# A decoder layer on one core: attention and feed-forward in one block, the first pair's front among the last turns of attention

## The chip, the core and the metric

The kernel runs on one core of a Trainium2 chip. Time is microseconds (us) of one execution on the device; the number compared is the median of the runs. A core has five engines with queues of their own: TensorE (PE in the rows; PEld is its loading of weights), VectorE (DVE), ScalarE (ACT), GpSimd (POOL) and SyncE (SP), which issues the transfers here. They meet only at semaphores: `need(engine, semaphore, count)` lets an engine wait there until the semaphore has that count.

## The reference, cut

16 sequences ("blocks") of 128 tokens and 256 channels go through three residual steps: causal attention with a second, geometric attention mixed in per head; a WKV recurrence whose keys are the normalised rows and whose values are the context `ctx_2048`; and a feed-forward part with a Hadamard rotation, 8-bit activations and ternary weights.

```python
x = x + attn_ref(layernorm(x), Wq, Wk, Wv, Wo, head_scales)       # 8 heads, 2 key heads, width 32
x = x + xattn_ref(16, 128, 256, time_decay, time_first, layernorm(x), ctx_2048)
x = x + ffn_ref(layernorm(x), w_gate, w_up, w_down)               # 256 -> 1024 -> 256

def h_bitlinear(x, w):
    xq = act_quant(fwht(x))         # Hadamard, then 127 / max|x| per token, rounded
    return einsum('bsh,oh->bso', xq, weight_quant(w))
# ffn: h_bitlinear(silu(gate) * up, w_down), gate and up by h_bitlinear of the same rows
```

## The kernel before, in words

Everything lies in SBUF: `x_res` holds all 16 blocks and is updated in place. The program is two blocks of code, one behind the other; at the change every engine waits for all the others.

The first block is attention and the WKV step (WKV is called context here). It runs in **turns**: in turn r, block r is in its first stage (f: transposes, L476, and q/k/v, L514), block r-1 in the second (m: scores L459 and L467, transposed scores L483 and L490, row maxima L639, transposed row data L496 to L499, geometric bounds L663 to L696, geometric scores L563), block r-2 in the third (b: value products L552, output product L586, residual L776, and then the statistics of the next normalisation), block r-3 in the fourth (c: normalisation L645, transposes L523, exponentials L383 and L386, products with values on GpSimd), and block r-4 in the last (d: two scans L652 and L656, additions L702 and L707, ScalarE's logarithm and exponential L415 and L418, product L771, transposes L597, residual L795). VectorE has a stage e ahead of these, one block further. The functions `body` of each engine spell out the order; `pipeline` calls them for 20 turns (VectorE 21), fully unrolled. Turns 16 to 19 have ever fewer stages: 17 has b, c and d, 18 c and d, 19 d alone.

ScalarE also turns the feed-forward weights ternary, a piece a turn (`ternary`, L341 and L344), and GpSimd takes roots by a power of -1/2 (L283, L327, L893). VectorE casts the large Hadamard matrix (L759) in turn 16.

The second block is the feed-forward part, in **passes** over 8 pairs of blocks. In pass r, pair r is in its front f, pair r-1 in m, r-2 in h, r-3 in b. The front is a chain over all engines: statistics on VectorE (L1170 to L1180), root and shift on GpSimd (L893, L895), normalised rows on ScalarE (L949), four transposes on TensorE (L1058), a copy on ScalarE (L959), the Hadamard transform (L1069, into `hx`), the largest value and its factors on VectorE (L1198 to L1213), rounding on ScalarE (L973, L977) and the diagonal of scales on GpSimd (L905), the way back on TensorE (L1089, L1092), and two copies on ScalarE (L988, L990). m is four column blocks j: gate and up products (L1008), the scaled gate on VectorE (L1111), the silu on ScalarE (L921, which has another activation table than the first block's exponentials), the product (L1120) and a sum and difference (L1125, L1126), split into a high part on ScalarE (L927) and a low one on GpSimd (L884). h is the 1024-wide Hadamard (L1022) and its maximum (L1133); b is the rounding (L932, L1031, L938), the down product (L1037) and the last residual (L1160). Pass 0 has the front of pair 0 only.

Of the kernel before, what the change touches and what calls it, by code (L numbers as in the profile page):

```python
# [14 lines left out]
P = 128  # L15
# [16 lines left out]
PEEL = 6  # L32
# [6 lines left out]
def need(eng, sem, count):  # L39

    if isinstance(count, int) and count <= 0:
        return
    eng.wait_ge(sem, count)
# [10 lines left out]
def upto(count, n):  # L54

    return min(count, n) if isinstance(count, int) else count


def pipeline(eng, n, stages, peeled, body):

    at = lambda u: (u, u % 2) if 0 <= u < n else None
    for r in range(peeled):
        body(*(at(r - s) for s in range(stages)))
    if peeled < n:
        with eng.Fori(peeled // 2, n // 2) as j:
            for half in range(2):
                body(*((2 * j + half - s, (half - s) % 2) for s in range(stages)))
    for r in range(n, n + stages - 1):
        body(*(at(r - s) for s in range(stages)))


def decoder_layer(nc, t, out):
    with ExitStack() as ctx:
# [31 lines left out]
        unround_c = sb("unround_c", [P, 1])  # L105

# [41 lines left out]
        with ExitStack() as ph:  # L148
# [4 lines left out]

            had_f = ph.enter_context(nc.sbuf_tensor("had_f", [P, FQ * 512], F32))
            w_junk = had_f[:, :]
            pick_f = ph.enter_context(nc.sbuf_tensor("pick_f", [40, H * P], F32))
            hs_in = ph.enter_context(nc.sbuf_tensor("hs_in", [P, REP], F32))
            head_mix = ph.enter_context(nc.sbuf_tensor("head_mix", [P, REP], F32))
            w_o_raw = ph.enter_context(nc.sbuf_tensor("w_o_raw", [P, REP, C], F32))
            st6 = ph.enter_context(nc.sbuf_tensor("a_st6", [P, NB, 6], F32))  # L160
            mv = ph.enter_context(nc.sbuf_tensor("a_mv", [P, NB, 2], F32))
            ve = ph.enter_context(nc.sbuf_tensor("a_ve", [P, NB], F32))
            rstd = ph.enter_context(nc.sbuf_tensor("a_rstd", [P, NB], F32))
# [6 lines left out]
            split_k = sa("a_split_k", [P, 2 * KVH * 4 * DH], F32R)  # L170
            dq = sa("a_dq", [P, 2 * H * 3])
            proj_d = sa("a_proj_d", [P, 2 * H])
            qkT = sa("a_qkT", [P, 1024], F32R)
# [10 lines left out]
            g_diag = sa("a_g_diag", [40, H * P])  # L184
            e_s = sa("a_e_s", [P, H * P])
            e_g = sa("a_e_g", [P, H * P])
# [41 lines left out]

            block = ph.enter_context(nc.Block())

# [587 lines left out]
        with ExitStack() as ph:  # L818
# [50 lines left out]
            def _(sp):  # L869
# [4 lines left out]
                for i in range(2):  # L874
                    sp.wait_ge(s_y[i], 16 * NP)

# [413 lines left out]
```

## Time and profile before

| what | value |
|---|---|
| three runs | 465.57, 466.85, 467.7 us; median 466.85 |
| the profiled execution | 464.53 us |
| its span, first to last instruction | 462.6 us |
| mean granted TensorE clock | 0.919 of 2.4 GHz |
| busy: TensorE, VectorE, ScalarE, GpSimd | 383.4, 331.9, 258.3, 152.0 us |

A row of a timeline has the start in us, the duration, engine, line of the program, operation and shapes, and in brackets how long the engine idled ahead of it and who ended that. Rows of several instructions (x4) give the first start and the time to the last end. A row of a table of stretches has from and to, the length, and the busy time (with instructions) of TensorE, its weight loads, VectorE, ScalarE and GpSimd; then the granted clock, the share of the transfer engines and GB/s. A clock of 0.50 is the lower of two levels, 1.2 GHz, and 1.00 is 2.4 GHz.

### The profile page before, as it was taken

The page shows a single profiled execution, that of the slowest core. Times are in us where ns is not written, and L with a number is a line of the kernel's source. Part 1 is how long each engine was busy: PE and PEld are TensorE (multiplying, and loading weights), DVE is VectorE, ACT ScalarE, POOL GpSimd, SP SyncE. Part 2 cuts the span into 40 slices and gives each one's busy share as a digit, 9 for nine tenths or more (in the row PEclk, how much of TensorE's full clock was granted, in tenths as well). Part 3 has the DMA queues.
Part 4 walks back from the last instruction along what each step waited for, and adds up shares of the span by engine and source line. Part 5 has one row for each costly group of instructions (what it writes and reads, how often), then busy time and mean ns, then how long its engine had stood idle before and what let it go on. Part 6 is the DMA issues. An engine that isn't in the chain of part 4 may idle for free. (4 is left out here: it accounts for less than half of the span.)

```text
span 462.6 us, 7493 instructions
## 1 busy us (share of the span) xinstructions
PE 383.4 (83%) x2290; PEld 252.8 (55%) x2306; DVE 331.9 (72%) x865; ACT 258.3 (56%) x482; POOL 152.0 (33%) x161
## 2 busy tenths in 40 slices
PE   2578899999999999999997714778999999989795
PEld 1345455565554665555643302456777777768573
DVE  4374769877779787797877362568889898897742
ACT  1133676456775667756575222555675585755642
POOL 1221345334553335443341111133433333332310
PEclk9776999999999999999998566569999999999998
DMA  8930003000000000000000000000000000000001
GB/s 233 314 118 1 0 2 104 11 13 11 14 0 13 12 13 13 12 2 11 13 13 11 0 1 2 0 0 0 3 13 11 24 11 14 13 12 24 11 25 34
DMA packets 13642, 13.14 MB, mean 28 GB/s; under 512 B 2004, under 2 KB 12884, under 8 KB 13476
## 3 DMA queue, kind: packets, MB, share of 16 engines
q1 hardware_dynamic: 13604, 12.67, 9.1%
q8 instruction: 19, 0.31, 0.3%
q14 instruction: 19, 0.16, 0.1%
HBM read 10.57 MB, written 2.10 MB: 27 GB/s over the span
## 5 line engine op out<-in xcount | busy, mean ns | idle before, releaser
L884 POOL TENSOR_TENSOR c_h_lo<-c_hb,c_h_hi 128x512 fp32r<-128x512 f32 x32 | 40.8, 1274 | 72.0 <-ACT c_h_hi L927 66.7
L1022 PE MATMUL wide<-had,c_h_hi 128*128 128x512 f32 x128 | 54.0, 422 | 7.5 <-ACT c_q2T L938 7.5
L1022 PE MATMUL wide<-had,c_h_lo 128*128 128x512 f32 x128 | 51.2, 400 | 0.0
L1008 PE MATMUL wide<-c_q_T,w_tern_all 128*128 128x256 bf16 x256 | 38.3, 292 | 8.3 <-DVE c_hh L1120 6.9
L296 POOL TENSOR_TENSOR a_qk<-a_rot_c,a_rot_s 128x320 f32<-128x320 f32 x16 | 15.4, 962 | 72.6 <-DVE a_rot_s L677 72.6
L302 POOL TENSOR_TENSOR a_split_q<-a_qk,a_split_q 128x256 fp32r<-128x256 f32 x16 | 33.8, 2111 | 15.3 <-ACT a_split_k L394 15.3
L921 ACT ACTIVATE c_sl<-c_z 128x512 f32<-128x512 f32 x32 | 20.1, 628 | 29.4 <-DVE c_z L1111 29.3
L776 DVE TENSOR_TENSOR x_res<-x_res,bank 128x256 f32<-128x256 f32 x16 | 6.8, 422 | 40.9 <-PE bank L597 36.2
L1008 PEld LDWEIGHTS wide<-c_q_T,w_tern_all 128*128 128x128 bf16 x256 | 24.2, 103 | 20.7 <-DVE c_hh L1120 9.3
L586 PE MATMUL bank<-w_o,a_att 128*128 128x256 f32 x128 | 33.3, 405 | 1.9 <-issue 1.1
L563 PE MATMUL wide<-a_g_diag,a_row_sb 40*128 40x512 f32 x64 | 31.7, 615 | 2.6 <-DVE a_g_diag L696 2.6
L1022 PEld LDWEIGHTS wide<-had,c_h_hi 128*128 128x128 f32 x128 | 24.6, 192 | 14.0 <-issue 9.3
L327 POOL TENSOR_TENSOR b_rstd<-b_ve,neg_half 128x1 f32<-128x1 f32 x16 | 8.8, 552 | 66.1 <-DVE b_ve L812 66.1
L1111 DVE SCALAR_TENSOR_TENSOR c_z<-wide,w_scale,c_s_row 128x512 f32<-128x512 f32 x32 | 23.8, 743 | 7.7 <-PE wide L1008 7.0
L1120 DVE TENSOR_TENSOR c_hh<-wide,c_sl 128x512 f32<-128x512 f32 x32 | 22.1, 691 | 9.2 <-ACT c_sl L921 9.2
L1133 DVE TENSOR_REDUCE c_am<-wide 128x1 f32<-128x1024 f32 x16 | 19.5, 1218 | 12.6 <-PE wide L1022 12.6
L586 PEld LDWEIGHTS bank<-w_o,a_att 128*128 128x128 f32 x128 | 24.1, 198 | 7.4 <-DVE a_att L765 2.5
L1022 PEld LDWEIGHTS wide<-had,c_h_lo 128*128 128x128 f32 x128 | 24.6, 192 | 4.5
L514 PE MATMUL bank<-w_qkv,a_xT 128*128 128x384 f32 x64 | 26.3, 537 | 0.6 <-ACT a_xT L352 0.6
L639 DVE TENSOR_REDUCE a_mx<-wide 128x8 f32<-128x1024 f32 x16 | 19.6, 1225 | 7.4 <-PE wide L467 7.2
L352 ACT COPY a_xT<-bank 128x256 f32<-128x256 f32 x16 | 6.0, 372 | 31.5 <-PE bank L476 31.5
L552 PE MATMUL bank<-a_e_s,ones 128*32 128x512 f32 x64 | 18.5, 654 | 5.4 <-issue 4.2
(168 smaller groups left out, 1009.6 us busy)
## 6 DMA issues: line engine op xcount, KB each, us to landing
x_res<-in_x SPq DMA_DIRECT2D x4, 512.0 KB, 6.2
b_vT<-in_ctxT SPq DMA_DIRECT2D x16, 128.0 KB, 2.3
out<-c_yo SPq DMA_DIRECT2D x16, 128.0 KB, 1.7
w_raw_all<-in_wg SPq DMA_DIRECT2D x1, 1024.0 KB, 7.4
w_raw_all<-in_wu SPq DMA_DIRECT2D x1, 1024.0 KB, 9.8
w_raw_all<-in_wd SPq DMA_DIRECT2D x1, 1024.0 KB, 12.3
had_f<-in_h SPq DMA_DIRECT2D x1, 1024.0 KB, 4.9
w_o_raw<-in_Wo SPq DMA_DIRECT2D x4, 128.0 KB, 6.3
```

Source lines behind the costliest of these rows:

```text
L302: nc.gpsimd.tensor_tensor(qv[:, :, 1, :], qk[p][:, 0:H * DH].rearrange("t (h d) -> t h d", h=H), qv[:, :, 0, :].bitcast(F32), ALU.subtract ...
L514: mm = nc.tensor.matmul(pj[:, 0:PW], xT[p][:, k * P:k * P + P], w_qkv[:, k, :], start=(k == 0), stop=(k == KC - 1))
L563: mm = nc.tensor.matmul(geo[:, g * 512:g * 512 + 512], k_row[p][:, :], g_diag[p][:, g * 512:g * 512 + 512], start=False, stop=True, skip_g ...
L586: mm = nc.tensor.matmul(wo_o, att[p][:, i * P:i * P + P], w_o[:, i, :], start=(i == 0), stop=(i == REP - 1))
L639: nc.vector.tensor_reduce(mx[p][:, :], scores[:, :].rearrange("t (h s) -> t h s", h=H), AX.X, ALU.max).then_inc(A["mx"], 1)
L884: nc.gpsimd.tensor_tensor(h_lo[p][:, j::FQ, :], hb[j % 2][:, :].rearrange("c (m t) -> c m t", m=2), h_hi[p][:, j::FQ, :].bitcast(F32), ALU ...
L921: nc.scalar.activation(sl[j % 2][:, :], z[j % 2][:, :], ACT.Silu).then_inc(D["sl"], 1)
L1008: mm = nc.tensor.matmul(dst[:, m * TOK:(m + 1) * TOK], w[:, k * FF + blk * P:k * FF + blk * P + P], q_T[p][:, k * TOK:(k + 1) * TOK], star ...
L1022: mm = nc.tensor.matmul(wide[:, 1 + i, m * 512:(m + 1) * 512], a[p][:, j + FQ * m, i * P:(i + 1) * P], had512[:, j, :], start=(j == 0 and ...
L1111: nc.vector.scalar_tensor_tensor(out=two_(z[j % 2][:, :]), in0=two_(gate), scalar=w_scale[:, 0:1], in1=spread(s_row[p][:, :], 1, 2), op0=A ...
L1120: nc.vector.tensor_tensor(hh[j % 2][:, :], up, sl[j % 2][:, :], ALU.mult).then_inc(D["h"], 1)
L1133: nc.vector.tensor_reduce(am2[p][:, c], wide[:, 1 + i, :], AX.X, ALU.max, apply_absolute_value=True).then_inc(D["am2"], 1)
```

## The change

The two blocks of code become one, and the buffers of the second lie beside those of the first. `woven` gives each engine's order: turns 0 to 17, pass 1, turn 18, pass 2, turn 19, passes 3 to 10. Pass 0 is gone; the front of pair 0 is spread by hand:

- VectorE: `pair_stats(0, 0)` ahead of turn 14, `pair_scale(0, 0)` behind turn 16, so ahead of turn 17's normalisation of block 14.
- GpSimd: `normal(0, 0)` behind turn 15, `scales(0, 0)` ahead of turn 17.
- ScalarE: `normed(0, 0)` behind turn 15, `turned(0, 0)` ahead of turn 16, `rounded(0, 0)` behind turn 16, `channels(0, 0)` behind turn 17.
- TensorE: `turn_x(0, 0)` in turn 16 behind the scores of block 15 and ahead of its transposed scores; `transformed(0, 0)` behind turn 16; `turned_back(0, 0)` in turn 17 ahead of the output product.

For pair 0, the transform and the way back have the free bank of the scores (`wide[:, 0]`) for a target. Blocks 14 and 15 have their context's product, transposes and residual taken out of turns 18 and 19: the product (`context_now`) stands on VectorE behind passes 2 and 3, the transposes (`context_out`) on TensorE ahead of passes 3 and 4, the residual (`context_add`) on VectorE within these. ScalarE loads the table of exponentials ahead of turns 18 and 19. The cast of the Hadamard matrix moves to turn 8. TensorE has 16 products of ones behind the q/k/v product of turn 0 and 8 behind the first geometric mask, in turn 1; nobody reads them. SyncE's loop of loads is unrolled, and its stores stand behind them.

```diff
+def woven(attention, pair, late=None):
+    for r in range(NB + 2):
+        attention(r)
+    pair(1)
+    attention(NB + 2)
+    pair(2)
+    if late:
+        late(NB - 2)
+    attention(NB + 3)
+    pair(3)
+    if late:
+        late(NB - 1)
+    for r in range(4, NP + 3):
+        pair(r)
...
+        hx = [wide[:, 0, 0:512]] + [bank[1]] * (NP - 1)
+        turn_qs = [wide[:, 0, 512:1024]] + [bank[0]] * (NP - 1)
...
 @block.gpsimd
+                def attention(r):
+                    if r == NB + 1:
+                        scales(0, 0)
+                    body(*slots(r, NB, 5))
+                    if r == NB - 1:
+                        normal(0, 0)
...
 @block.scalar
+                def attention(r):
+                    if r >= NB + 2:
+                        nc.scalar.preload_act_table_set("natural_log_exp_and_others")
+                    if r == NB:
+                        turned(0, 0)
+                    body(*slots(r, NB, 5))
+                    if r == NB - 1:
+                        normed(0, 0)
+                    if r == NB:
+                        rounded(0, 0)
+                    if r == NB + 1:
+                        channels(0, 0)
...
 @block.tensor
+                def turn_x(u, p):
+                    need(pe, D["xn"], 2 * (u + 1))
+                    need(pe, D["srow"], u)
+                    need(pe, A["att"], NB - 2 if u == 0 else NB)
...
+                def idle_work(dst, n):
+                    for _ in range(n):
+                        nc.tensor.matmul(dst[:, 0:P], ones[:, :], ones[:, :], start=True, stop=True)
...
+                    if m is not None and m[0] == NB - 1:
+                        turn_x(0, 0)
...
+                        if u == 0:
+                            idle_work(scoresT, 16)
...
+                        if u == 0:
+                            idle_work(turn, 8)
...
+                    if b is not None and b[0] == NB - 1:
+                        turned_back(0, 0)
...
+                def attention(r):
+                    body(*slots(r, NB, 5))
+                    if r == NB:
+                        transformed(0, 0)
+                def pair(r):
+                    if r in (3, 4):
+                        context_out(NB - 5 + r, (r + 1) % 2)
+                    feed(*slots(r, NP, 4))
...
 @block.vector
+                    if f is not None and f[0] in (3, 4):
+                        context_add(NB - 5 + f[0], (f[0] + 1) % 2)
...
+                def attention(r):
+                    if r == NB - 2:
+                        pair_stats(0, 0)
+                    body(*slots(r + 1, NB, 6))
+                    if r == NB:
+                        pair_scale(0, 0)
+                attention(-1)
+                woven(attention, lambda r: feed(*slots(r, NP, 4)), lambda u: context_now(u, u % 2))
...
-                    if f is None and m is not None and b is not None:
+                    if e is not None and e[0] == 9:
 
                         dve.wait_ge(s_ffc, 2 * 16)
                         nc.vector.tensor_copy(had512[:, :, :].rearrange("p a b -> p (a b)"), had_f[:, :]).then_inc(s_cst, 1)
```

## Rows read from the trace of the kernel before

**Rows 1.** The page: TensorE's busy tenths and its granted clock, 40 slices.
```profile
PE   2578899999999999999997714778999999989795
...
PEclk9776999999999999999998566569999999999998
```

**Rows 2.** Table of stretches: feed-forward passes.
```profile
330.00:400.00 70.00, 64.51 (x416) 51.95 (x415) 61.64 (x156) 47.84 (x74) 24.00 (x26) 1.00 0.04 12
```

**Rows 3.** Timeline of TensorE, from turn 16 on, and one transform at full clock.
```profile
239.07 1.11 PE L467 MATMUL wide<-a_qkT 64*128 64x128 f32 x16
...
249.06 1.98 PE L563 MATMUL wide<-a_g_diag,a_row_sb 40*128 40x512 f32 x4
...
256.20 0.69 PE L523 MATMUL wide<-ident,b_xn 128*128 128x128 f32 x2 [3.02 <-DVE b_xn L645]
...
264.85 0.64 PE L597 MATMUL bank<-ident,b_y 128*128 128x128 f32 x2
...
282.82 3.55 PE L1069 MATMUL bank<-had,c_x3T 128*128 128x256 f32 x8 [0.67 <-ACT c_x3T L959]
...
291.82 2.98 PE L1008 MATMUL wide<-c_q_T,w_tern_all 128*128 128x256 bf16 x12 [0.68 <-ACT c_q_T L988]
...
317.77 1.96 PE L1069 MATMUL bank<-had,c_x3T 128*128 128x256 f32 x8
```

**Rows 4.** Timeline of TensorE in turns 0 and 1.
```profile
17.09 0.72 PE L576 MATMUL wide<-ident_r,a_split_q 128*128 128x128 f32 x4 [4.36 <-POOL a_split_k L306]
...
19.42 1.03 PE L459 MATMUL wide<-mask_ts,ident_b 128*128 128x512 bf16 x2 [1.10 <-ACT a_qkT L427]
...
31.50 1.98 PE L563 MATMUL wide<-a_g_diag,a_row_sb 40*128 40x512 f32 x4 [2.42 <-DVE a_g_diag L696]
```

**Rows 5.** Table of stretches: the first gap, and dense stretches of turns 1 and 2.
```profile
12.75:17.09 4.34, 0.00 (x1) 0.04 (x1) 3.19 (x15) 0.92 (x3) 2.26 (x3) 0.92 1.16 240
...
19.42:26.50 7.08, 7.08 (x35) 4.51 (x36) 1.48 (x2) 1.10 (x4) 0.00 (x0) 0.50 1.06 368
...
35.77:43.50 7.73, 7.73 (x36) 4.85 (x37) 2.57 (x7) 3.13 (x6) 1.10 (x1) 0.50 0.01 2
```

**Rows 6.** Timeline of VectorE, turns 15 to 19 and pass 0.
```profile
226.25 1.23 DVE L639 TENSOR_REDUCE a_mx<-wide 128x8 f32<-128x1024 f32 x1
...
243.12 0.45 DVE L663 TENSOR_TENSOR_SCAN a_cmax<-a_row_sb 8x128 f32<-8x128 f32 x1
...
247.91 1.21 DVE L759 CAST had<-had_f 128x2048 fp32r<-128x2048 f32 x1
...
272.76 0.69 DVE L652 TENSOR_TENSOR_SCAN b_sum_e<-decay,b_e_in 128x258 f32<-128x258 f32 x1
...
275.34 0.43 DVE L771 TENSOR_TENSOR b_y<-b_num,b_inv 128x256 f32<-128x256 f32 x1 [0.65 <-DVE b_num L707]
...
287.82 0.68 DVE L1213 TENSOR_SCALAR c_fac<-c_rs,w_scale 128x2 f32<-128x2 f32 x1
```

**Rows 7.** Timeline of GpSimd: the powers for block 13 and for pair 0.
```profile
240.67 0.55 POOL L327 TENSOR_TENSOR b_rstd<-b_ve,neg_half 128x1 f32<-128x1 f32 x1 [3.40 <-DVE b_ve L812]
...
278.81 0.70 POOL L893 TENSOR_TENSOR c_rstd<-c_ve,neg_half 128x2 f32<-128x2 f32 x1 [1.45 <-DVE c_ve L1180]
```

**Rows 8.** Timeline of ScalarE: turn 18, pass 0, table load, gate activations of passes 1, 2.
```profile
268.98 0.63 ACT L383 ACTIVATE b_e_in<-wide,guard_n 128x128 f32<-128x128 f32 x2 [8.14 <-PE wide L523]
...
270.45 0.42 ACT L418 ACTIVATE b_inv<-b_ln 128x256 f32<-128x256 f32 x1
...
279.89 1.09 ACT L949 ACTIVATE c_xn<-x_res,c_shift,c_rstd 128x256 f32<-128x256 f32 x2 [4.64 <-POOL c_shift L895]
...
292.06 1.28 ACT L921 ACT_TABLE_LOAD   x1
293.75 0.63 ACT L921 ACTIVATE c_sl<-c_z 128x512 f32<-128x512 f32 x1 [0.41 <-DVE c_z L1111]
...
310.86 0.63 ACT L921 ACTIVATE c_sl<-c_z 128x512 f32<-128x512 f32 x1 [0.48 <-DVE c_z L1111]
```

More of the change, by code:

```diff
@@ L54, in upto, with slots @@
 def upto(count, n):
[L56 to L69, printed above, removed]
+    return min(count, n)
+def slots(r, n, stages):
+    return [(r - s, (r - s) % 2) if 0 <= r - s < n else None for s in range(stages)]
+def woven(attention, pair, late=None):
[12 more added lines that the diff above has]
+        pair(r)
 def decoder_layer(nc, t, out):
@@ new lines, in attention @@
+                def attention(r):
[10 more added lines that the diff above has]
+                        channels(0, 0)
+                woven(attention, lambda r: feed(*slots(r, NP, 4)))
@@ new lines, in hadamard @@
+                def hadamard(u, p, i, half):
+                    need(pe, D["hi"], 4 * u + 2 * half + 2)
+                    need(pe, D["lo"], 4 * u + 2 * half + 2)
+                    if half == 0:
+                        need(pe, B["en"], KC * NB)
+                        need(pe, D["q2T"], 2 * (u - 1) + i + 1)
+                    for j in (2 * half, 2 * half + 1):
+                        for m in range(2):
+                            for part, a in enumerate((h_hi, h_lo)):
+                                mm = nc.tensor.matmul(wide[:, 1 + i, m * 512:(m + 1) * 512],
+                                                      a[p][:, j + FQ * m, i * P:(i + 1) * P], had512[:, j, :],
+                                                      start=(j == 0 and part == 0), stop=(j == FQ - 1 and part == 1))
+                    if half == 1:
+                        mm.then_inc(D["had"], 1)
@@ L599, in _, with feed @@
[L599 removed]
+                    if d is not None and d[0] < NB - 2:
+                        context_out(*d)
+                def feed(f, m, h, b):
+                    done = NP if f is None else f[0]
+                    if m is not None:
+                        gate_up(*m, 0)
+                    if h is not None:
+                        hadamard(*h, 0, 0)
+                    if m is not None:
+                        gate_up(*m, 1)
+                    if h is not None:
+                        hadamard(*h, 0, 1)
+                    if f is not None:
+                        turn_x(*f)
+                    if m is not None:
+                        gate_up(*m, 2)
+                    if f is not None:
+                        transformed(*f)
+                    if b is not None:
+                        turn2(*b, 1)
+                        if f is None:
+                            need(pe, D["srow"], NP)
+                            need(pe, D["yo"], 2 * b[0] - 1)
+                        project_down(*b, 0)
+                    if h is not None:
+                        hadamard(*h, 1, 0)
+                    if m is not None:
+                        gate_up(*m, 3)
+                    if f is not None:
+                        turned_back(*f)
+                    if h is not None:
+                        turn2(*h, 0)
+                        hadamard(*h, 1, 1)
+                    if b is not None:
+                        need(pe, D["qm"], 2 * (done if f is None else done + 1))
+                        need(pe, D["yo"], 2 * b[0])
+                        project_down(*b, 1)
@@ L601, in _ @@
+                def attention(r):
[6 more added lines that the diff above has]
+                    feed(*slots(r, NP, 4))
+                woven(attention, pair)
             @block.vector
```

752 lines of the change are left out of this document (353 added, 399 removed).

## The prediction

> **What bounds the kernel now.** I read the page's slices first: the line of granted clocks, one digit for a fortieth of the span (11.6 us), has, besides its last digit, two stretches below 9, the second to fourth digit and the 22nd to 27th, and in the later one TensorE's busy share is down to 1 tenth once [rows 1]. In the feed-forward passes behind it TensorE works 64.5 of 70 us and VectorE 61.6 [rows 2]: there two engines are nearly full, and work put on VectorE is paid almost in full, while the hole between the two halves is nearly free. TensorE's order of time through the hole [rows 3]: turn 16 begins at 238.55 (its scores, L467, at 239.07), turn 17 at 256.20, its last product (L597) ends at 265.5, then two context blocks, the change of blocks and the whole front of pair 0 stand alone, and the first gate and up products of pass 1 start at 291.82. These 26.3 us are what the change goes for. At the start TensorE idles twice: 4.36 us ahead of L576 and 2.42 us ahead of L563 [rows 4].
>
> **The start.** The change puts 16 idle products of 128 columns into the first gap and 8 into the second. One costs an eighth of the eight instructions of L1069: 0.44 us by the half-clock row (3.55 us), 0.245 by the full-clock one (1.96 us) [rows 3], so 16 take 3.9 to 7.1 us from 12.75, and end at 16.6 or 19.8; L576 could start at 17.09 [rows 4]. In the gap the granted clock averaged 0.92 and was at 0.50 when L576 came [rows 5]: it was at its upper level (2.4 GHz) first and fell after TensorE had idled. I take 16.6: hidden, with 2.7 us lost as the other bound. The 8 take 2.0 of the 2.42 us: hidden.
> What they may give back: the next dense stretch, 19.42 to 26.50, is 7.08 us of solid TensorE work at 0.50, and its twin in turn 2 is 7.73 us [rows 5]. At 2.4 GHz they would shrink by 3.5 and 3.9. But then the row maxima on VectorE (L639, 1.23 us [rows 6]), which half-speed products cover now, stand in the open once per turn: 7.4 - 2.4 = **5.0 us less**. Bounds: 2.7 us more (full price, no clock) and 7.4 less.
>
> **Turns 8 and 14.** The cast of the large Hadamard matrix (1.21 us [rows 6]) moves on VectorE from turn 16 to turn 8, ahead of the attention product: 0 to 1.2 us there; I take +0.5, since VectorE has idle time later in the turn. The statistics of pair 0 go ahead of the row maxima of turn 14: GpSimd waited 1.45 us for them ahead of 278.81 [rows 7], and VectorE didn't idle ahead of the maxima at 226.25 [rows 6], so **+1.3** (0 to 1.5).
>
> **The seam, turn 16.** Here a new wait comes in. TensorE's turn now asks for the first pair's normalised rows right behind the scores, which end at 240.2 [rows 3]. GpSimd makes their 1/sigma only behind its own last step of turn 15, the power for block 13 at 240.67, 0.55 us [rows 7]; then 0.70 for its own power, 0.3 for the shift (242.2), then ScalarE's two activations, 1.09 us [rows 8]: 243.4. TensorE stands **3.2 us** in the middle of turn 16, with the whole score-transposed group, the transposes of rows, the context and value products queued behind it; VectorE's scans and geo bounds wait for those in turn. An idle of 3.02 us ahead of L523 at 256.20 was followed by products at the lower clock [rows 1, 3], so I let the transposes (1.1 us) and the next 2.7 us of products run at half speed: the rows reach ScalarE at 247.5. VectorE starts its running maxima (L663) at 248.0 instead of 243.12 and ends the diagonal product some 4.0 us later, at 252.0 [rows 6]. L563 starts at 252.1 instead of 249.06, only 3 us late, since it had waited for half-speed value products before [rows 3]. The rest of the turn (L563, L586, L597: 4.4 us) ends at 256.5, against 253.2.
>
> **The seam, turn 17.** Pair 0's transform follows (1.96 us at full clock, 3.55 at half [rows 3]), to 258.4, and covers the gap of 3.02 us. But its scaling is on VectorE ahead of block 14's normalisation, and has to wait for the transform: 2.1 us from the transform's end (286.37) to the end of the last factor (288.50) [rows 3, 6]. So block 14's transposes, TensorE's first step of turn 17, come at 260.9 (2.1 and 0.4 behind 258.4) and not at 256.2. Behind them: the value products, pair 0's way back, the output product and L597. Before, this turn took 9.3 us from L523 to the end of L597 (265.5), all at half clock, with 0.8 of idling [rows 3]; the way back adds about 1.6 at half clock (an estimate: its product with the diagonal is a quarter of L1069's 3.55, 0.9, and its four transposes are at most as much again). So 10 us at half, 5.0 at full; after another 2.5 us of idling I take half for the first part and full for the rest, 7.1. **Pass 1 starts at 268** instead of 291.8, between 266 and 271: **23.8 us less**. ScalarE has the quantised rows ready by then: the way back is done about 265, and the two copies take one microsecond.
>
> **Pass 1.** Its products follow dense work now, so part of it runs at full clock: the pair's transform alone is 1.6 us shorter [rows 3]. Against that VectorE comes 0.35 us later to the first gate. **1.0 less** (3 less to 1 more).
>
> **Turns 18 and 19 in the passes.** They were in the hole at no cost and now lie on full engines. VectorE's part of turn 18 is the normalisation, two scans and two additions, 0.4 and 1.9 us (272.76 until L771 could have gone, 274.69); of turn 19 the same 1.9; and each block's product with the inverse and its residual 0.8 more [rows 6]. ScalarE's part: each turn loads the exponent table and the next gate activation loads its own again, 1.28 us each [rows 8], four loads more, plus activations: 1.9 us in turn 18 (268.98 to 270.87), 0.85 in turn 19 [rows 8]. Turn 18 on ScalarE comes between its last cast of pass 1 (about 310.4) and the activation that began at 310.86 [rows 8]: 1.28 + 1.9 + 1.28 put that to about 315, and the up product of the second column block waits for it. Some of these 4.1 us is VectorE's statistics of the pair, which went there anyway: **+3.5**. Turn 19 in the same way: VectorE +2.3, ScalarE +3.4, **+2.8**. At the head of pass 4 TensorE waits for block 15's product, which VectorE does only behind its own last steps of pass 3: **+1.5**. Together 7.8, with 5 (half the loads hidden under VectorE) and 11 (none, and GpSimd late) as bounds. SyncE's loads of context are unrolled and keep their order, and its stores of results come behind them as before: nothing.
> The gate activation behind the one table load in the passes idled 0.41 us, put down to its data [rows 8]; the trace prices a switch at 1.28 us, and at most 1.7. The Trainium skill (ScalarE: Activation LUTs, "What ACT_TABLE_LOAD costs") gives 1.283 us for the load, as the row has it, but adds about 1.38 us of drain, some 2.66 us for every switch; by it, four switches would cost up to 5.5 us more than by the rows. No stretch of this trace can show the drain, since ScalarE had nothing to do there.
>
> **The sum**, against the profiled execution (464.53 us; 1.9 around the span of 462.6): -5.0 + 0.5 + 1.3 - 23.8 - 1.0 + 7.8 = -20.2, so 444.3. That execution lies 2.3 us under the median of the three runs, 466.85; I carry the same distance: **446.6**, taken as 446.5.
>
> **Rivals.**
> *The seam keeps its clock.* If the filler transform keeps TensorE at 2.4 GHz, turn 17 takes 5 us and pass 1 gains its 3 us: 442.5. For it: TensorE has one long gap less. Against: two gaps of 3.2 and 2.5 us remain. 0.15.
> *The idle products buy nothing.* The waits for qkT (1.1 us ahead of L459, twice [rows 4]) stay, and the clock may fall in them; with the 16 at half speed L576 is late. Start 0 instead of -5.0, or +2.7: 451.5 to 454. 0.13.
> *ScalarE becomes the bound of passes 2 and 3.* If each of the four switches stops ScalarE for longer than its 1.28 us, by as much again as the load, 4 x 1.3 = 5 us come on top: 452. The Trainium skill's drain, cited above, would do that. For it: gate activations gate VectorE in these passes. Against: no row. 0.13.
> *The front isn't spread, only moved.* If each of its steps holds up the turn that it is in for its own length, only the hole of turns 18 and 19 is won, 265.5 to about 277.4 or 11.9 us [rows 3, 7] instead of 23.8: 458.5. 0.04.
> *Slower: the passes at half clock.* With TensorE interrupted at the heads of passes 2, 3 and 4 it could stay at 1.2 GHz through them. A pass is 17 to 18 us of TensorE work in some 19 (64.5 of 70 [rows 2]), so each at 0.50 costs about 16 us; from 1.3 such passes on the gain is gone, with two the time is 478. Against: the granted clocks are back at 9 from the 28th digit on, though passes interrupt TensorE there too [rows 1]. 0.04.
>
> **How the numbers follow.** Forecast 0.50, rivals 0.15, 0.13, 0.13, 0.04, 0.04, no net change 0.01. From 440 (first rival with the start's better bound) to 453 holds the forecast, the first, and most of the second and third: about 8 in 10. A difference under 0.5% (2.3 us) can't be told from none here. Faster by more 0.95, within 0.01, slower 0.04.
>
> **What would show it.** In the changed profile: L576 of turn 0 no later than 17.5 us, and the stretch after L459 at a clock over 0.8; in turn 16 an idle of about 3 us ahead of the four transposes of pair 0, put down to ScalarE's normalised rows; block 14's transposes waiting 2 to 3 us more for VectorE; the gate products of pass 1 29 us after the scores of block 15 instead of 52.8; four table loads more, and passes 2, 3 and 4 longer by 3.5, 2.8 and 1.5 us than before. The prediction is wrong if passes 2 to 4 lose more than 11 us, if pass 1 starts later than 33 us after those scores, or if the first three turns are not shorter.

## Result, and the profile after

The changed kernel took 452.54 us (median of four executions), the kernel before 466.21 beside it, some 14 us less where 20 were forecast; 446.5 us stood as the time, and 452.54 lies near the upper end of the forecast range, 440 to 453. One of the four executions, at 464.25 us, lay well above the rest and is left out of the ratio, which is 0.967 with a 95% interval of 0.957 to 0.977; the other three took 447.05 to 453.16. The first profile is of the execution at 464.25 us. Against a second profile of the same kernel (449.92 us, span 448.1) it is 6.7 us longer in four turns, 3.6 at the start and 3.7 in the seam, each time with products at the lower clock. The rows below are from the second profile, unless they are said to be of the first.

TensorE's busy tenths and granted clock in 40 slices, the second profile first, as in [rows 1]:

```profile
PE   2889899999989999998996876588888998999794
...
PEclk9997999999999999999997698798999999999898
```

and those of the first:

```profile
PE   2889899999989999999896976597988999989795
...
PEclk9876999998998989998998578779899999999898
```

The hole of [rows 1] (busy tenth 1) is gone. The granted clock of the second and third slice is 9 in the second profile and 8 and 7 in the first. TensorE's timeline through the start and the seam, as in [rows 3, 4]:

```profile
12.19 5.27 PE L742 MATMUL wide<-ones 128*128 128x128 f32 x32
17.21 0.54 PE L886 MATMUL wide<-ident_r,a_split_q 128*128 128x128 f32 x4
19.19 0.60 PE L763 MATMUL wide<-mask_ts,ident_b 128*128 128x512 bf16 x2 [1.10 <-ACT a_qkT L585]
19.72 1.11 PE L771 MATMUL wide<-a_qkT 64*128 64x128 f32 x16
...
32.61 1.97 PE L771 MATMUL wide<-a_qkT 64*128 64x128 f32 x16
...
133.62 1.99 PE L898 MATMUL bank<-w_o,a_att 128*128 128x256 f32 x8 [0.79 <-DVE a_att L1227]
...
211.86 0.27 PE L802 MATMUL wide<-ident,a_mx 128*8 128x128 f32 x1 [1.36 <-DVE a_mx L1101]
...
237.15 0.59 PE L763 MATMUL wide<-mask_ts,ident_b 128*128 128x512 bf16 x2
...
242.40 1.11 PE L709 MATMUL bank<-ident,c_xn 128*128 128x128 f32 x4 [3.62 <-ACT c_xn L480]
...
247.63 1.97 PE L837 MATMUL wide<-a_m_row,pick_neg 40*128 40x128 f32 x8 [0.95 <-DVE a_m_row L1129]
...
254.06 2.09 PE L873 MATMUL wide<-a_g_diag,a_row_sb 40*128 40x512 f32 x4
...
258.14 1.89 PE L724 MATMUL wide<-had,c_x3T 128*128 128x256 f32 x8
262.52 0.44 PE L831 MATMUL wide<-ident,b_xn 128*128 128x128 f32 x2 [2.49 <-DVE b_xn L1107]
...
268.23 1.04 PE L668 MATMUL wide<-c_q_T,w_tern_all 128*128 128x256 bf16 x8
271.06 0.61 PE L668 MATMUL wide<-c_q_T,w_tern_all 128*128 128x256 bf16 x4 [1.80 <-DVE c_z L997]
```

L742 are the idle products (16 of them show as x32), L763 the masks that begin a turn, L709 pair 0's transposes, L724 its transform, L831 the key transposes, L668 gate and up products. Turn 16 begins at 237.15 (before at 238.55) and the gate products come 31.08 us later; before, 291.82 - 238.55 = 53.27. From here on "behind turn 16's begin" means behind that L763.

The passes are told best by the way back of each pair (L1089 before, L734 after), one per pass. Timeline of TensorE before:

```profile
289.58 0.61 PE L1089 MATMUL bank<-ident_b,c_qb 128*128 128x128 bf16 x4 [3.20 <-ACT c_qb L977]
306.67 0.63 PE L1089 MATMUL bank<-ident_b,c_qb 128*128 128x128 bf16 x4
323.71 0.39 PE L1089 MATMUL bank<-ident_b,c_qb 128*128 128x128 bf16 x4
342.41 0.39 PE L1089 MATMUL bank<-ident_b,c_qb 128*128 128x128 bf16 x4
361.49 0.39 PE L1089 MATMUL bank<-ident_b,c_qb 128*128 128x128 bf16 x4
```

and after:

```profile
264.74 0.40 PE L734 MATMUL wide<-ident_b,c_qb 128*128 128x128 bf16 x4
282.72 0.39 PE L734 MATMUL bank<-ident_b,c_qb 128*128 128x128 bf16 x4
302.46 0.39 PE L734 MATMUL bank<-ident_b,c_qb 128*128 128x128 bf16 x4
324.46 0.39 PE L734 MATMUL bank<-ident_b,c_qb 128*128 128x128 bf16 x4
345.30 0.39 PE L734 MATMUL bank<-ident_b,c_qb 128*128 128x128 bf16 x4
```

From one to the next, in us: 17.09, 17.04, 18.70, 19.08 before; 17.98, 19.74, 22.00, 20.84 after. Step by step, the forecast beside this execution (us; a step is the change of the interval that holds it):

| step | forecast | measured | from |
|---|---|---|---|
| start, to turn 3's begin | -5.0 | -4.3 | 53.87 to 49.61 |
| turn 8, the cast | +0.5 | +1.0 | 14.25 to 15.26 |
| turn 10 | 0 | +0.5 | 14.15 to 14.62 |
| turn 14, the statistics | +1.3 | +1.4 | 14.15 to 15.53 |
| seam, turn 16's begin to gate products | -23.8 | -22.2 | 53.27 to 31.08 |
| pass 1, gate products to way back of pair 1 | -1.0 | -0.4 | 14.85 to 14.49 |
| passes 2 to 4 | +7.8 | +7.8 | three intervals above |
| behind pair 7's way back | 0 | +1.6 | 43.5 to 45.1 |
| span | -20.2 | -14.5 | 462.6 to 448.1 |

The last stretch has the change's work nowhere in it. Its granted clock was 0.91 and 0.92 from 410 to 420 and from 420 to 430 us, where the same work before (426 to 446 us) had 1.00. In the profiles of the runs below that share this code it takes 42.9 to 45.2 us, so the 1.6 lies within what one execution differs from another.

### The profile page after: what moved, and what is told of

Read it like the earlier page. It is cut to its first block and busy times, and to the rows that moved or that the text cites. A ratio compares the mean times of both kernels' runs of the same rounds, so it can differ in the third digit from the quotient of the medians.

```text
span 462.4 us, 7523 instructions
## 1 busy us (share of the span) xinstructions
PE 398.0 (86%) x2354; PEld 263.9 (57%) x2354; DVE 330.9 (72%) x866; ACT 263.1 (57%) x486; POOL 153.8 (33%) x160
## 5 line engine op out<-in xcount | busy, mean ns | idle before, releaser
L683 PE MATMUL wide<-had,c_h_hi 128*128 128x512 f32 x128 | 56.0, 438 | 8.5 <-ACT c_q2T L472 8.0
L683 PE MATMUL wide<-had,c_h_lo 128*128 128x512 f32 x128 | 52.9, 414 | 0.0
L668 PE MATMUL wide<-c_q_T,w_tern_all 128*128 128x256 bf16 x256 | 36.9, 286 | 8.2 <-DVE c_hh L1006 6.4
L898 PE MATMUL bank<-w_o,a_att 128*128 128x256 f32 x128 | 39.6, 464 | 2.4 <-DVE a_att L1227 1.3
L683 PEld LDWEIGHTS wide<-had,c_h_hi 128*128 128x128 f32 x128 | 25.7, 201 | 15.8 <-issue 10.7
L668 PEld LDWEIGHTS wide<-c_q_T,w_tern_all 128*128 128x128 bf16 x256 | 23.9, 102 | 18.3 <-DVE c_hh L1006 8.5
L873 PE MATMUL wide<-a_g_diag,a_row_sb 40*128 40x512 f32 x64 | 33.5, 645 | 0.8 <-DVE a_g_diag L1158 0.8
L898 PEld LDWEIGHTS bank<-w_o,a_att 128*128 128x128 f32 x128 | 27.8, 228 | 8.9 <-issue 2.7
L683 PEld LDWEIGHTS wide<-had,c_h_lo 128*128 128x128 f32 x128 | 25.8, 202 | 5.0
L997 DVE SCALAR_TENSOR_TENSOR c_z<-wide,w_scale,c_s_row 128x512 f32<-128x512 f32 x32 | 23.8, 743 | 4.7 <-PE wide L668 3.3
L580 ACT ACTIVATE a_e_g<-wide 128x1024 f32<-128x1024 f32 x16 | 16.4, 1028 | 11.8 <-PE wide L873 11.8
## 6 DMA issues: line engine op xcount, KB each, us to landing
w_raw_all<-in_wd SPq DMA_DIRECT2D x1, 1024.0 KB, 12.5
```

The costliest lines, as they stand in the source:

```text
L668: mm = nc.tensor.matmul(dst[:, m * TOK:(m + 1) * TOK], w[:, k * FF + blk * P:k * FF + blk * P + P], q_T[p][:, k * TOK:(k + 1) * TOK], star ...
L683: mm = nc.tensor.matmul(wide[:, 1 + i, m * 512:(m + 1) * 512], a[p][:, j + FQ * m, i * P:(i + 1) * P], had512[:, j, :], start=(j == 0 and ...
L873: mm = nc.tensor.matmul(geo[:, g * 512:g * 512 + 512], k_row[p][:, :], g_diag[p][:, g * 512:g * 512 + 512], start=False, stop=True, skip_g ...
L898: mm = nc.tensor.matmul(wo_o, att[p][:, i * P:i * P + P], w_o[:, i, :], start=(i == 0), stop=(i == REP - 1))
L997: nc.vector.scalar_tensor_tensor(out=two_(z[j % 2][:, :]), in0=two_(gate), scalar=w_scale[:, 0:1], in1=spread(s_row[p][:, :], 1, 2), op0=A ...
```

## The experiments

Ratios are to the kernel before in the same call, with 95% intervals; the changed kernel itself came to 0.969 (0.963 to 0.975) in the first.

**The same kernel again.** No edit.

> The changed kernel once more, unchanged, for a profile of another of its executions. Theory A: the 464 us of the profiled execution is the design's own time plus falls of the granted clock in four turns that are steady otherwise (2.7, 2.2, 1.7 and 1.5 us) and in pass 3 and 4; another execution then has these turns at 14.3 us and a span near 447 to 451, and what it loses at the start (0.7 us gained where 5.0 were forecast), in turn 16 (29.0 us from the scores of block 15 to the first key transposes of turn 17, 22.3 forecast) and in pass 1 (18.8, 16.1 forecast) stands there as before. Rival B: those losses too come and go with the execution: then turn 16 to 17 takes some 22 us and the start gains 5 us in this one.

It took 452.09 us (median), and its profile is the one above. The four long turns are gone (turns 4 to 13 take 14.1 to 14.3 us, but for turn 8's 15.26 and turn 10's 14.62). The start kept its clock here: in the first profile turn 3 began at 53.20, here at 49.61. Turn 16's begin to turn 17's key transposes is 25.4, between the two theories: 29.0 in the first profile holds 3.7 us of a longer half clock. Pass 1 is the same in both (18.3 and 18.0 us from way back to way back). So A for the steady turns and pass 1, B for the start and part of the seam.

**Without the idle products.**

```diff
-                            idle_work(scoresT, 16)
-                            idle_work(turn, 8)
```

> The changed kernel without the 16 and the 8 idle products. As the prediction had it (they hold the clock through turns 1 and 2): 5.0 us slower than the changed kernel in the same call. Rival, by the trace of the changed kernel (granted clock at 0.50 again from 20 to 26 us, turn 2 begins at 34.70 us instead of 35.77): they buy what the first turn shows, 0.5 to 1 us, and the rest of the two turns is the same with them and without; then the two kernels lie within 1.5 us.

0.977 (0.971 to 0.982), so 0.8% or 3.6 us slower than with them: less than the 5.0 forecast, and more than the rival's 0.5 to 1 us. Why the first profile showed only 0.7 us is seen in its timeline of TensorE:

```profile
12.16 3.98 PE L742 MATMUL wide<-ones 128*128 128x128 f32 x32
16.74 0.52 PE L886 MATMUL wide<-ident_r,a_split_q 128*128 128x128 f32 x4 [0.59 <-POOL a_split_k L381]
...
18.70 0.60 PE L763 MATMUL wide<-mask_ts,ident_b 128*128 128x512 bf16 x2 [1.10 <-ACT a_qkT L585]
```

There the 16 products ran at full clock, ended at 16.1 and left 0.59 us open, and the clock fell at 19.8. In the second profile some of them ran at half clock (5.27 us in place of 3.98), L886 followed without a gap, 0.5 us later, and the clock held until 32.6. The nine profiles with this start fall into the same two groups: turn 3 begins at 49.2 to 50.7 us where no gap was left, and at 52.6 to 53.2 where one was. That the gap is the cause isn't shown: where there was none, some of the 16 products had run at half clock, and no run separates the two. In one of these (the run without the table switches, 50.68) the clock fell all the same, from 20.3 to 24 us.

**Pair 0's transposes later in turn 16.**

```diff
-                    if m is not None and m[0] == NB - 1:
-                        turn_x(0, 0)
...
+                        if u == NB - 1:
+                            turn_x(0, 0)
```

The new place is behind the transposes of the three row pieces. ScalarE's copy moves along, and the value products of that turn wait for it.

> In turn 16 the transposes of pair 0 (turn_x) go behind the transposes of the three row pieces instead of ahead of the masks of the transposed scores, and ScalarE's copy of them behind that turn's copies of rows and values. Theory A: TensorE's 3.62 us of idle time ahead of them, which GpSimd's power and ScalarE's normalisation set, are what lets the granted clock fall to half from 252 to 272 us; then the wait is gone, the clock holds, and the scores of block 15 stand 10 to 12 us nearer to the key transposes of turn 17 (29.0 us in the changed kernel): 8 to 12 us faster in all. Rival B: the half clock has other causes (turn 16 waits elsewhere too), and only the wait itself goes: 2 to 4 us faster. Rival C: turn 16 hangs on VectorE's and ScalarE's rows, which come no sooner: within 1 us.

0.966 (0.960 to 0.972). In the trace the seam is 4.2 us shorter (key transposes 21.1 us behind turn 16's begin instead of 25.4, gate products 26.8 instead of 31.1); this execution lost 3.5 at its start and 5 in turns 7, 8 and 10, so that the ratios of the two kernels, 0.966 and 0.969, can't be told apart. Rival B, by the trace: the wait shrinks from 3.62 to 1.55 us, the half clock stays. The products behind L709 are at half rate:

```profile
251.04 0.66 PE L709 MATMUL bank<-ident,c_xn 128*128 128x128 f32 x4 [1.55 <-ACT c_xn L480]
...
252.22 1.96 PE L837 MATMUL wide<-a_m_row,pick_neg 40*128 40x128 f32 x8
```

**Pair 0's scaling behind block 14's normalisation.**

```diff
-                    if r == NB:
-                        pair_scale(0, 0)
...
+                        if u == NB - 2:
+                            pair_scale(0, 0)
```

> VectorE's pair_scale of pair 0 goes behind the normalisation of block 14 instead of ahead of it. Theory A (the prediction's): the wait of 2.49 us ahead of the key transposes of turn 17 goes, and the first gate products of pass 1 come 1.5 to 2.5 us sooner. Rival B: the wait moves to where the factors are needed (ScalarE's rounding, then the way back), and gate products come within 0.5 us of where they were; the total is the same within 1 us. Rival C: slower, if the rounding of pair 0 then holds ScalarE's exponentials of block 14 back (up to 2 us).

0.974 (0.968 to 0.979), slower than the changed kernel if anything, and in the trace by 2.4 us: gate products 33.5 us behind turn 16's begin. Rival C, as far as one trace shows it. Timeline of TensorE in turn 17:

```profile
261.50 0.44 PE L831 MATMUL wide<-ident,b_xn 128*128 128x128 f32 x2 [1.28 <-DVE b_xn L1107]
...
264.51 0.40 PE L734 MATMUL wide<-ident_b,c_qb 128*128 128x128 bf16 x4 [0.72 <-ACT c_qb L496]
...
267.47 3.17 PE L898 MATMUL bank<-w_o,a_att 128*128 128x256 f32 x8 [2.07 <-DVE a_att L1229]
```

1.2 us is won at L831. But ScalarE stands in its rounding of pair 0 until 262.68 (3.83 us, put down to c_qs), its exponentials and the inverse for block 15 come behind that, and L898 waits 2.07 us for the division, after which the clock is down. The order that the prediction had complained of is the better one.

**Without the table switches.**

```diff
-                    if r >= NB + 2:
-                        nc.scalar.preload_act_table_set("natural_log_exp_and_others")
...
-    nc.scalar.activation(..., ACT.Exp, bias=guard_n[:, k:k + 1])
+    nc.scalar.activation(..., ACT.Exp if u < NB - 1 else ACT.Identity, bias=guard_n[:, k:k + 1])
```

The other exponential of the keys and the logarithm and exponential of the context's division are changed in the same way.

> The four switches of ScalarE's table in passes 2 and 3 are taken out of the changed kernel: in turns 18 and 19 the exponentials of block 15 and the logarithms and exponentials of the last two context divisions become Identity, which leaves those two blocks' context wrong and their time otherwise as it is. Theory A (the prediction's, 1.28 us a load, most of it on the path in pass 2, little in pass 3): 2.5 to 4 us faster than the changed kernel, nearly all of it in passes 2 and 3. Rival B: the loads lie in ScalarE's waits: within 1.5 us. Rival C: a switch costs 2.66 us (load and what runs out ahead of it): 7 to 10 us faster.

0.963 (0.958 to 0.969). The intervals from way back to way back decide: 18.91, 19.75, 21.49, 20.85 us, against 17.98, 19.74, 22.00, 20.84 with the switches. The first lies ahead of all four switches and differs by the clock of pass 1; in the other three the switches cost 0.5 us in all: rival B. (The total is 2.5 us lower by the ratio, but the key transposes of turn 17 came 21.8 us behind turn 16's begin in this profile instead of 25.4, ahead of anything that the edit touches; more on this below.) Turn 18 of the changed kernel, timeline of ScalarE:

```profile
286.52 1.28 ACT L639 ACT_TABLE_LOAD   x1
287.82 0.63 ACT L541 ACTIVATE b_e_in<-wide,guard_n 128x128 f32<-128x128 f32 x2
...
289.29 0.42 ACT L576 ACTIVATE b_inv<-b_ln 128x256 f32<-128x256 f32 x1
289.73 1.28 ACT L454 ACT_TABLE_LOAD   x1
291.02 0.63 ACT L454 ACTIVATE c_sl<-c_z 128x512 f32<-128x512 f32 x1
```

Each activation starts 0.01 to 0.02 us behind its load, and the second load 0.02 us behind the activation ahead of it: 1.28 us and nothing more. The Trainium skill (ScalarE: Activation LUTs, "What ACT_TABLE_LOAD costs") adds a drain of about 1.38 us; this trace shows none.

**Turns 18 and 19 ahead of pass 1.**

```diff
-    for r in range(NB + 2):
+    for r in range(NB + 4):
         attention(r)
-    pair(1)
-    attention(NB + 2)
...
+    for r in range(1, NP + 3):
+        pair(r)
```

> Turns 18 and 19 (the keys of block 15, the last two context sums, their transposes and their adding to the stream) go back ahead of pass 1; the front of pair 0 stays spread over turns 14 to 17. Theory A (the prediction's sum with that part put back): the gate products of pass 1 come 11 to 14 us later than in the changed kernel, pass 1 is 2 to 3 us shorter, passes 2 to 4 together 5 to 7 us shorter: 3 to 6 us slower. Rival B: what the weaving saves ahead of pass 1 it gives back in passes 1 to 4: within 1.5 us. Rival C: in the thin turns 18 and 19 the granted clock falls, and pass 1 begins at half clock: 8 us slower or more.

0.973 (0.966 to 0.980). Gate products come 42.4 us behind turn 16's begin (11.3 later), and the intervals of passes 2 to 4 are 16.80, 18.71 and 19.11: 8.0 us shorter. From pair 0's way back to pair 7's it is 140.5 us against 138.2: weaving the two turns into the passes buys 2.3 us by this count, 1.8 by the ratios. That is between A's 3 to 6 and B's 1.5, and less than the runs' totals can settle.

**The seam filled.** The late transposes, and

```diff
+                    if u == 0:
+                        idle_work(c_turn, 6)
...
+                        if u >= NB - 2:
+                            idle_work(kt, 9)
...
+                        n_idle = {(0, 1, "g"): 6, (0, 1, "u"): 4, (0, 3, "u"): 8}.get((u, j, s_done), 0)
+                        idle_work(wide[:, 1, :], n_idle)
```

The first stands in turn_x ahead of its wait for the normalised rows, the second ahead of the key transposes' wait, the third in gate_up ahead of the wait for a free bank.

> The late transposes of pair 0 (as in the run that moved them) and, beside that, idle products in TensorE's waits of turn 16, turn 17 and pass 1: 6 ahead of pair 0's transposes, 9 ahead of the key transposes of block 14 and of block 15, 6, 4 and 8 ahead of three gate and up products of pass 1. Compared stretch by stretch with the run without them (scores of block 15 to the key transposes of turn 17: 21.1 us; to the first gate products of pass 1: 26.8 us; to those of pass 2: 45.3 us). Theory A: waits are what lets the granted clock fall there; filled, it holds and the whole stretch takes 40 to 42 us. Rival B: it falls for what lies ahead of the fill (turn 16 has no projection and no block to turn): 44 to 46 us. Rival C: the idle products stand in front of what comes in time: over 46 us.

446.01 us, 0.952 (0.947 to 0.958), against 0.969 of the changed kernel. Theory A: key transposes 18.2 us behind turn 16's begin, gate products 23.9, those of pass 2 41.3. Table of stretches (the clock is the third number from the end) from turn 16 to pass 2; the changed kernel first:

```profile
242.40:253.50 11.10, 9.82 (x44) 5.09 (x45) 5.05 (x10) 5.44 (x13) 1.41 (x2) 0.50 0.04 12
...
270.00:286.00 16.00, 7.91 (x42) 5.54 (x42) 12.68 (x31) 8.43 (x16) 5.92 (x7) 0.86 0.00 1
```

and filled:

```profile
242.00:254.00 12.00, 11.13 (x76) 6.62 (x75) 8.85 (x19) 7.91 (x17) 3.29 (x5) 1.00 0.04 12
254.00:282.00 28.00, 23.48 (x171) 18.43 (x170) 21.49 (x58) 16.49 (x32) 8.79 (x11) 1.00 0.00 1
```

**Filled, but the transposes where they were.**

```diff
-                        idle_work(c_turn, 6)
+                        idle_work(c_turn, 14)
```

> The changed kernel with pair 0's transposes where they were, ahead of the masks in turn 16, and the waits of the seam filled with idle products (14 ahead of those transposes instead of 6; the others as in the run with the filled seam). Theory A: the half clock behind the waits, not the waits, is the larger part of what the seam lost: the clock holds, from the scores of block 15 to the key transposes of turn 17 21 to 22.5 us (25.4 in the changed kernel, 18.2 with the transposes moved as well), to the gate products of pass 2 44.5 to 46 us (49.6 and 41.3). Rival B: filled waits hold the clock only together with the move: within 1 us of the changed kernel's 25.4 and 49.6.

0.953 (0.949 to 0.957). Key transposes 22.3, gate products 28.0, those of pass 2 45.4 us behind turn 16's begin: A by its times. Of the 8.3 us by which the filled and moved seam beats the changed kernel's 49.6, the fills are 4.2 and the move 4.1. But the clock did not hold all through: behind a wait that was not filled, the value products of turn 16 ran at half rate. Timeline of TensorE:

```profile
250.79 1.11 PE L844 MATMUL wide<-a_m_row,pick_neg 40*128 40x128 f32 x8 [1.16 <-DVE a_m_row L1136]
251.83 1.04 PE L867 MATMUL bank<-a_e_s,ones 128*32 128x512 f32 x2
...
255.92 1.98 PE L880 MATMUL wide<-a_g_diag,a_row_sb 40*128 40x512 f32 x4
```

VectorE's diagonal product, which L880 needs, was ready at 254.2. So some 1.7 of the move's 4.1 us are the clock too (an estimate, from these two times): with the move that wait is 0.30 us, and the products behind it keep their rate.

**The start filled as well.**

```diff
-                            idle_work(scoresT, 16)
+                            idle_work(scoresT, 20)
...
-                            idle_work(turn, 8)
+                            idle_work(turn, 11)
...
+                        if u < 2:
+                            idle_work(turn, 5 + u)
```

> The run with the filled seam, and more idle products at the start: 20 instead of 16 behind the first projection, 5 and 6 ahead of the scores of turns 1 and 2, 11 instead of 8 ahead of the geometric products of turn 1. Theory A: at the start too it is the remaining waits (0.6 to 0.7 us ahead of the first turned block and 1.10 us ahead of the first scores, where the clock then fell at 19.8 us; in the executions in which the idle products covered the first of them it did not fall until 32 us) that let the clock go: turn 3 begins at 49.6 us or sooner (46 to 48 if turn 2 holds too) in place of 53.1, 3.5 to 6 us faster than the run without. Rival B: the clock falls for other reasons in some executions and not in others: turn 3 begins at 53 us, no faster. Rival C: the added products stand in the way: the start later than 53.2 us.

0.945 (0.941 to 0.950). Turn 3 begins at 48.05 us, and the clock is up in turn 1 and in turn 2 as far as its output product, which ran at half rate (3.34 us, at 44.87). Table of stretches, as above; in the changed kernel 32 to 40 us was at 0.57:

```profile
19.00:26.00 7.00, 6.92 (x54) 4.60 (x53) 3.90 (x8) 1.63 (x6) 0.89 (x1) 1.00 1.05 390
32.00:40.00 8.00, 7.71 (x65) 4.47 (x63) 5.72 (x18) 4.39 (x11) 2.19 (x3) 1.00 0.00 0
```

**The cast in quarters on VectorE, and on ScalarE.** The second stands at the end of ScalarE's front stage, on top of the filled seam and start.

```diff
-                    if e is not None and e[0] == 9:
+                    if e is not None and 9 <= e[0] <= 12:
-                        nc.vector.tensor_copy(had512[:, :, :].rearrange("p a b -> p (a b)"), had_f[:, :])
+                        nc.vector.tensor_copy(had512[:, q, :], had_f[:, q * 512:(q + 1) * 512])
```

```diff
+                        if 9 <= u <= 12:
+                            nc.scalar.copy(had512[:, q, :], had_f[:, q * 512:(q + 1) * 512])
```

> The cast of the Hadamard matrix (1.74 us on VectorE in turn 8) is cut into four pieces of 128x512 in turns 8 to 11. Theory A: VectorE has some 0.5 us to spare in a turn, so the whole cast costs turns 8 and 10 together 1.4 us (15.26 and 14.62 us where a steady turn takes 14.27) and the pieces cost nothing: turns 8 to 11 are 14.3 us each. Rival B: VectorE has nothing to spare and the sum is the same, each of the four turns 0.3 to 0.5 us longer. Against the changed kernel: 1.4 us faster under A, the same under B; the spread of runs may hide either, so the turns of the trace decide.

> The run before it (filled seam, filled start), and the cast of the Hadamard matrix in four pieces on ScalarE, at the end of turns 9 to 12, instead of whole on VectorE. Theory A: VectorE sets the length of turns 8 and 10 (15.26 and 14.62 us), ScalarE, busy 60% of its time, has room: those turns take 14.27 us and turns 9 to 12 as well, 1.3 us faster than the run without. Rival B: ScalarE's chain is on the path of a turn too, and each piece adds its 0.5 us or so: 0.5 us slower or more.

On VectorE, turns 8 to 11 took 14.45, 14.46, 14.80 and 14.45 us: 0.2 each, and turn 10 keeps its 0.4 (0.964, 0.957 to 0.971). The sum of the four is 58.16 against 58.43 whole: rival B. On ScalarE the wait for the division (0.79 us ahead of L898) is gone from turn 8, which took 15.84 us all the same, since its output product ran at half rate (3.36 us); turns 9 and 11 to 13 take 14.3 us: A. Turn 10 still takes 14.63, so that is not the cast; in the changed kernel VectorE stands 0.30 us there ahead of the row maxima and waits for nothing that the trace shows. 443.76 us, 0.942 (0.938 to 0.946): the lowest of the series, though not told apart from the run before it (0.945), and 1.7% to 3.7% under the changed kernel by the two intervals' ends.

**The order before, filled.** Idle products alone in the kernel before, at its own waits.

```diff
+                            idle_work(scoresT, 20)
...
+                            idle_work(kt, 11)
...
+                            idle_work(scoresT, 10)
...
+                            idle_work(wide[:, 1, :], 16)
```

> The kernel before, its order untouched, with idle products alone: at the start as in the run with the filled start (20, 5 and 6, 11), 11 ahead of the key transposes of blocks 14 and 15, 10 ahead of the last two context transposes, 16 and 11 ahead of the two steps of pair 0's front that TensorE waits for, and 2, 6, 4 and 8 ahead of gate and up products of pass 1. It asks what the change's new order is worth once the clock holds in either order. Theory A: fills and order are worth about the same: the start gains 5 to 6 us, the seam 4 to 7 us (its products at half clock, some 10 us of them, halve), 454 to 458 us where the kernel before has 466 to 468; the new order with the same fills stays 10 to 12 us ahead (0.945 of before). Rival B: the clock was nearly the whole gain, and this kernel lies within 4 us of the changed order with fills (below 450). Rival C: in the thin turns 17 to 19 fills of this size do not hold the clock, and the gain is the start's alone: 460 to 463.

454.34 us, 0.976 (0.968 to 0.984): theory A. With nothing reordered, idle products win 2.4%, about 11 us; the new order without any idle products won 2.3% (0.977, above). Alone, the two are worth about the same. Gate products come 45.4 us behind turn 16's begin (53.3 unfilled, 23.9 with the new order filled). The new order still leads by 3%, from 0.976 to 0.945.

## Why the prediction was right, and where it was off

**Right:** the mechanisms and their places. The new wait in turn 16 was forecast at 3.2 us and is 3.62, for the reason given. Timeline of GpSimd, as in [rows 7]:

```profile
239.27 0.55 POOL L402 TENSOR_TENSOR b_rstd<-b_ve,neg_half 128x1 f32<-128x1 f32 x1 [3.41 <-DVE b_ve L1267]
239.79 0.70 POOL L354 TENSOR_TENSOR c_rstd<-c_ve,neg_half 128x2 f32<-128x2 f32 x1
240.57 0.65 POOL L356 TENSOR_TENSOR c_shift<-c_mneg,c_rstd 128x2 f32<-128x2 f32 x1
```

The shift took 0.65 us, not 0.3. The wait of block 14's transposes for VectorE is 2.49 us (2.5), turn 14's is 1.36 (1.3), and passes 2, 3 and 4 are longer by 2.70, 3.30 and 1.76 (3.5, 2.8, 1.5): 7.8 as summed.

**Off, in size.** The seam's -23.8 is -22.2. The step that was too small is "I let the transposes (1.1 us) and the next 2.7 us of products run at half speed": the granted clock was 0.50 for 11 us, to 253.5, the products that subtract the row maxima (L837, 1.97 us) and the value products with it. VectorE ended its diagonal product at 251.04, 13.9 us behind turn 16's begin, close to the forecast 13.45; but TensorE reached L873 at 16.9 and not 13.55. So TensorE at half clock, not VectorE, ended that turn, 3 us late. Turn 17 gave 1.4 back (5.7 us from L831 to the gate products, 7.1 forecast).

How long the half clock lasts behind the same wait differs from one execution to the next. Seven profiles have this order up to there and wait 3.6 us ahead of pair 0's transposes. In five of them the products behind are at half rate for 11 us; in the first profile for 19, to 272 us, and its seam was -18.5; in the run without the table switches for 3.8, just as the prediction let it. Timeline of TensorE in that run (its lines are numbered two less):

```profile
248.60 0.66 PE L707 MATMUL bank<-ident,c_xn 128*128 128x128 f32 x4 [3.62 <-ACT c_xn L480]
...
253.36 1.10 PE L835 MATMUL wide<-a_m_row,pick_neg 40*128 40x128 f32 x8 [0.95 <-DVE a_m_row L1127]
```

There the geometric scores came 13.5 us behind turn 16's begin (forecast 13.55) and the key transposes 21.8 (22.35). So the chain that the prediction laid out is right where the clock does what it assumed, and the size of that term can't be read from one execution. Filled and with the transposes moved, the seam holds 1.00, which the rival "the seam keeps its clock" had asked for, and the change by itself doesn't bring.

The start's -5.0 is -4.3 here, -0.7 in the first profile and -3.6 by the runs without it. The prediction took "hidden" as enough. What went with the loss in four of the nine profiles is a gap behind the fill: 16 products at full clock are 3.9 us in a gap of 4.4 to 4.6. Its sign "the stretch after L459 at a clock over 0.8" holds in the second profile (1.00 to 26 us) and not in the first (0.50 from 20 to 26 us).

The cast took 1.74 us in turn 8 and not the 1.21 of [rows 6]; 0.7 of that was hidden. Turn 10's 0.5 was not forecast and stays unexplained. Pass 1's -1.0 is -0.4: TensorE idles there, and the clock fell again (0.86 from 270 to 286); with the waits filled that stretch takes 13.6 us instead of 14.49.

**Right by luck.** Passes 2 to 4 came out at 7.8, but the sum put much of it on ScalarE's table switches, and they are worth 0.5. By the trace TensorE idles 5.2 us more in these passes than before (10.1 against 4.9) and is busy 2.5 us more. The new idling is mostly waits for VectorE at the woven steps: 2.64 us ahead of block 15's key transposes, 1.94 and 1.15 ahead of the last two context transposes. That VectorE's own work is the price was not tried alone.

**The rivals.** That the idle products buy nothing is what the first profile shows alone, and not the runs (3.6 us). ScalarE as the bound falls with the 0.5 us of four switches. A front only moved would have left the seam at -11.9, passes at half clock would show in the intervals: neither does.

**The rest.** About 3 of the missing 5.7 us lie in stretches with a term (start 0.7, seam 1.6, pass 1 0.6) and go with the clock there, 1.6 lie at the end, where the change has nothing, 1.0 in turns 8 and 10.

## What to carry to other kernels

A wait of TensorE can cost more than itself, in products at half clock behind it: here 3.62 us of idle time were followed by 11 us at 0.50, in other executions by 3.8 and by 19. So count a new wait with the dense work behind it at half speed, as a range and not as one number. Fill waits that can't be removed with idle products up to the moment at which the data comes, and look whether a gap is left. Before a large reordering, fill the waits of the old order first: here that won 2.4%, as much as the new order without idle products (2.3%), and the two together, with the transposes moved, 5.5%.

## What the hardware showed that was not expected

The clock also falls where the order gives no cause that the traces show. The first profile of the changed kernel has four turns that are about 1.7 us longer than in the second, and in each it is the output product that ran at half rate. Two of them, timeline of TensorE:

```profile
107.82 3.33 PE L898 MATMUL bank<-w_o,a_att 128*128 128x256 f32 x8
...
214.00 3.65 PE L898 MATMUL bank<-w_o,a_att 128*128 128x256 f32 x8
```

In the other steady turns it takes 1.96 to 1.99. TensorE was busy for 12.3 to 12.5 of the 13.3 to 13.4 us ahead of these two, and nothing was late. Such falls are in nine of the twelve profiles of the experiments too, one to four in each from turn 3 on, and not in the profile of the kernel before, whose times range from 461.7 to 474.6 us all the same. They recur in the same places: the three profiles with the filled start, one of them of the order before, have the output product of turns 2, 5 and 8 at half rate, each of them, at 44.9 to 45.4, 88.4 to 89.3 and 133.1 to 133.9 us. What brings them on stays open.
